# Gated graph phase: node rows from three split fp32r products, tiles in pairs, 512-column elementwise instructions

## The reference, cut to what matters

```
t   = relu(nf @ W1.T + b1)            # one row of 256 per node: "rows"
s   = segment_sum(t[src], dst)        # sum over the incoming edges: "messages"
m   = s @ W2.T + deg * b2             # W2 is folded into W_ih ahead of the steps
r,z = sigmoid(...), n = tanh(...)     # GRU gates from m and nf: "gates"
nf  = (1 - z) * n + z * nf
```

## Time and profile before

| | |
|---|---|
| device time, three runs | 4059.73, 4059.72, 4056.88 us; median 4059.72 us |
| span of the profiled execution, first to last instruction | 4057.3 us |
| PE busy | 3711.8 us, 91% of the span |
| DVE, ACT, POOL busy | 62%, 38%, 19% |
| granted clock of PE, mean over the span | 0.959 of full speed |

### The profile page before, as it was taken

One profiled execution on the slowest core, in us unless ns is written; L12 is line 12 of the kernel. 1 busy time (PEld: TensorE's weight loads), 2 busy tenths in 40 slices (PEclk: granted clock), 3 DMA queues, 4 the chain that ended last, 5 costly groups with the idle time before them and its releaser, 6 DMA issues. The chain is left out here.

```text
span 4057.3 us, 61050 instructions
## 1 busy us (share of the span) xinstructions
PE 3711.8 (91%) x18981; PEld 3087.0 (76%) x18981; DVE 2525.8 (62%) x5060; ACT 1533.3 (38%) x3578; POOL 758.0 (19%) x614
## 2 busy tenths in 40 slices
PE   5996879999999999999998799787999999779996
PEld 2554459989899899898997688655888888758884
DVE  7774755555555555555554555544777777577775
ACT  0363211121211211212112544334888886135553
POOL 0000000000000000000000200003888885012221
PEclk9997989999999999999999899898999999779998
DMA  1364112222222222222221211012333332411113
GB/s 41 64 102 87 48 50 78 87 67 85 76 79 86 74 80 87 67 85 76 79 85 40 66 30 31 13 41 61 93 93 93 94 93 68 177 44 35 38 35 116
DMA packets 297743, 288.61 MB, mean 71 GB/s; under 512 B 101485, under 2 KB 272847, under 8 KB 296806
## 3 DMA queue, kind: packets, MB, share of 16 engines
q1 hardware_dynamic: 233867, 208.29, 17.8%
q0 software_dynamic: 56576, 66.41, 6.4%
q10 hardware_dynamic: 7002, 10.15, 0.7%
HBM read 241.89 MB, written 42.47 MB: 70 GB/s over the span
## 5 line engine op out<-in xcount | busy, mean ns | idle before, releaser
L974 PE MATMUL bank<-a_wide,parts 125*128 125x448 f32 x4200 | 871.5, 367 | 0.1
L974 PEld LDWEIGHTS bank<-a_wide,parts 125*128 125x128 f32 x4200 | 785.7, 188 | 77.2 <-issue 10.1
L2205 POOL DMA_INDIRECT rows<-h_dram,src_t x400 | 493.5, 1234 | 124.1 <-DVE prod L2394 87.3
L2321 ACT ACTIVATE hot<-eq,ea 125x80 f32<-125x80 f32 x1600 | 413.2, 350 | 0.0
L949 POOL TENSOR_TENSOR nf_g<-nf,nf_g 128x896 fp32r<-128x896 f32 x42 | 94.5, 2249 | 1525.4 <-ACT nf_g L1112 1525.4
L1024 DVE CAST a_wide<-a_cols 125x2240 fp32r<-125x2240 bf16 x210 | 274.5, 1324 | 156.5 <-PE bank L974 141.0
L983 PE MATMUL bank<-nf_g,whh 128*128 128x448 f32 x1512 | 339.6, 369 | 0.0
L983 PE MATMUL bank<-msg,wc 128*128 128x448 f32 x1512 | 338.9, 368 | 0.0
L2247 PEld LDWEIGHTS bank<-prod,hot 125*80 125x80 f32 x2400 | 294.6, 150 | 54.1 <-issue 0.7
L2247 PE MATMUL bank<-prod,hot 125*80 125x128 f32 x2400 | 327.9, 273 | 0.0
L1117 ACT ACTIVATE msg<-bank 128x448 fp32r<-128x448 f32 x84 | 41.1, 542 | 702.6 <-PE bank L974 702.6
(11 more groups left out here) (431 smaller groups left out, 5894.4 us busy)
## 6 DMA issues: line engine op xcount, KB each, us to landing
a_cols<-a_dram SPq DMA_DIRECT2D x210, 546.9 KB
a_dram<-a_cols SPq DMA_DIRECT2D x15, 1250.0 KB, 10.9
w<-in_w SPq DMA_DIRECT2D x4, 2728.0 KB
deg_bc<-deg_dram SPq DMA_DIRECT2D x42, 224.0 KB, 6.1
gate_bc<-gate_dram SPq DMA_DIRECT2D x42, 224.0 KB, 3.2
rows<-h_dram,src_t POOLq DMA_INDIRECT x400, 4.2
w<-y_rows SPq DMA_DIRECT2D x12, 512.0 KB, 10.1
w<-in_w SPq DMA_DIRECT2D x5, 1024.0 KB
```

Of the source, the lines that this page charges most:

```text
L974: ins = nc.tensor.matmul(p_msg[f][:, 0:GW], parts[0:SPB, m, c * HB + k, f * 128:(f + 1) * 128], a_wide[u % 2][0:SPB, k, :], start=(c == 0 ...
L2205: nc.gpsimd.indirect_dma_start(out=rows[n % ITC][:, :], out_offset=None, in_=h_dram, in_offset=bass.IndirectOffsetOnAxis(ap=src_t[:, n:n + ...
L2321: ins = nc.scalar.activation(hot[:, q % 2, j, m, :], eq[:, q % 2, j, :], ACT.Copy, scale=ea4[:, q * UC + j, m:m + 1])
```

## The change

Row tiles are handled in pairs: ten pairs of early tiles, and three late entries (two pairs and the last tile alone). For each pair

- ACT copies the two tiles' columns of `nf` to fp32r (`nf_r[0]`, 128x500), POOL subtracts this from `nf` (`nf_r[1]`), and PE makes the three-term product of `nf_r` and a `w1` that is split into `w1[0]` and `w1[1]` in the weights phase. PE has 6 fp32r products of 256 columns for a tile, where it had 2 fp32 products;
- bias, relu and remainder are one instruction each for both tiles, 512 columns wide instead of 256.

`nf_r` and `t_raw` have two buffers, each for a pair. PE now waits for POOL's part (`row_low`) where it waited for `nf` itself. In ACT's list the copy of pair i stands ahead of the relu of pair i-1. The core of the diff:

```diff
@@ norm_and_gate_weights, the ends of POOL's and ACT's lists
+                pool.wait_ge(rest_in, START + 80)
+                pool.wait_ge(w1_high, START + 1)
+                nc.gpsimd.tensor_tensor(w1[1][:, :, :], w1_raw[:, :, :], w1[0][:, :, :], ALU.subtract)
...
+                act.wait_ge(rest_in, START + 80)
+                nc.scalar.activation(w1[0][:, :, :], w1_raw[:, :, :], ACT.Copy).then_inc(w1_high, 1)
@@ gated_graph, pairs
+    early, late = ([(k, min(k + 2, b)) for k in range(a, b, 2)] for a, b in ((0, EARLY * HB), (EARLY * HB, KT)))
@@ POOL
+                    def rows(s, some):
+                        for a, b in some:
+                            i = s * NPAIR + pairs.index((a, b))
+                            pool.wait_ge(row_high, START + i + 1)
+                            nc.gpsimd.tensor_tensor(nf_r[1][:, i % 2, :, 0:(b - a) * SPB], nf[:, :, a * SPB:b * SPB],
+                                                    nf_r[0][:, i % 2, :, 0:(b - a) * SPB], ALU.subtract).then_inc(row_low, 1)
...
+                        if g == 0:
+                            rows(s, late)
+                        if g == NGG - 1 and s < STEPS - 1:
+                            rows(s + 1, early)
@@ PE
-                            pe.wait_ge(nf_done, START + (s - 1) * NGG + min((k * SPB + SPB - 1) // GW + 1, NGG))
+                            pe.wait_ge(row_low, START + i + 1)
                             pe.wait_ge(t_sum, START + i - 1)
-                            for c in range(KD):
-                                ins = nc.tensor.matmul(p_t[i % 2][0:SPB, 0:D], nf[:, c, k * SPB:(k + 1) * SPB], w1[:, c, :],
-                                                       start=(c == 0), stop=(c == KD - 1))
+                            for h in range(b - a):
+                                terms = [(w1[m], nf_r[o], c) for m, o in ((0, 0), (0, 1), (1, 0)) for c in range(KD)]
+                                for j, (w_m, x_o, c) in enumerate(terms):
+                                    ins = nc.tensor.matmul(p_t[i % 2][0:SPB, h * D:(h + 1) * D], x_o[:, i % 2, c, h * SPB:(h + 1) * SPB],
+                                                           w_m[:, c, :], start=(j == 0), stop=(j == len(terms) - 1))
                             ins.then_inc(t_mm, 1)
@@ DVE
-                            dve.wait_ge(t_high, START + i - 3)
-                            dve.wait_ge(t_low, START + i - 3)
-                            nc.vector.tensor_tensor(t_raw[0:SPB, i % 4, :], p_t[i % 2][0:SPB, 0:D], b1_bc[0:SPB, :], ALU.add).then_inc(t_sum, 1)
+                            dve.wait_ge(t_high, START + i - 1)
+                            dve.wait_ge(t_low, START + i - 1)
+                            nc.vector.tensor_tensor(t_raw[0:SPB, i % 2, 0:b - a, :],
+                                                    p_t[i % 2][0:SPB, 0:(b - a) * D].rearrange("p (h d) -> p h d", d=D),
+                                                    b1_bc[0:SPB, :].rearrange("p (o d) -> p o d", o=1).broadcast_to((SPB, b - a, D)),
+                                                    ALU.add).then_inc(t_sum, 1)
@@ ACT
+                            act.wait_ge(nf_done, START + (s - 1) * NGG + min((b * SPB - 1) // GW + 1, NGG))
+                            act.wait_ge(t_mm, START + i - 1)
+                            nc.scalar.activation(nf_r[0][:, i % 2, :, 0:(b - a) * SPB], nf[:, :, a * SPB:b * SPB], ACT.Copy).then_inc(row_high, 1)
+                            if (a, b) != some[0]:
+                                relu(i - 1)
+                        relu(i)
+
+                    def relu(i):
+                        a, b = pairs[i % NPAIR]
+                        act.wait_ge(t_sum, START + i + 1)
+                        nc.scalar.activation(parts[0:SPB, 0, a:b, :], t_raw[0:SPB, i % 2, 0:b - a, :], ACT.Relu).then_inc(t_high, 1)
```

More of the change, by code:

```diff
@@ L168, in build @@
             ctx_w = ExitStack()
-            w1_g = sb(ctx_w, "w1_g", [128, KD, D])
+            w1_g = [sb(ctx_w, f"w1_g{m}", [128, KD, D], F32R) for m in range(PARTS)]
             wc = [sb(ctx_w, f"wc{m}", [128, KD, 3 * D], F32R) for m in range(PARTS)]
@@ L912, in gated_graph, with pairs_to @@
     EARLY = (NGG - 1) * GW // SPB // HB
+    early, late = ([(k, min(k + 2, b)) for k in range(a, b, 2)] for a, b in ((0, EARLY * HB), (EARLY * HB, KT)))
+    pairs = early + late
+    NPAIR = len(pairs)
+    def pairs_to(tile):
+        return next(i for i, (a, b) in enumerate(pairs) if b >= tile) + 1
     w1, wc, whh, b1_bc, b2, bih, bhh, bsum, b2c = gate_w
@@ L916, in gated_graph @@
         r_t, t_t, n_t, z_t = (shared[:, m * KD * GW:(m + 1) * KD * GW].rearrange("p (k n) -> p k n", k=KD) for m in range(4))
-        t_raw = sb(ctx, "t_raw", [128, 4, D])
+        t_raw = sb(ctx, "t_raw", [128, 2, 2, D])
+        nf_r = [sb(ctx, f"nf_r{m}", [128, 2, KD, 2 * SPB], F32R) for m in range(PARTS)]
         parts = sb(ctx, "parts", [128, PARTS, KT, D], F32R)
@@ L1002, in gates @@
                             gate(p_z, 1, f, False, wc, msg, True).then_inc(z_mm, 1)
-                    rows(0, range(EARLY * HB))
+                    rows(0, early)
                     for n in range(GR):
@@ L1008, in _ @@
                             if g == 0 and c == EARLY - 1:
-                                rows(s, range(EARLY * HB, KT))
+                                rows(s, late)
                             messages(s, n, c)
                         if g == NGG - 1 and s < STEPS - 1:
-                            rows(s + 1, range(EARLY * HB))
+                            rows(s + 1, early)
                         gates(n)
@@ L1100, in _, with rows @@
                 with act.If(crowded < 1):
-                    def rows(s, tiles):
-                        for k in tiles:
-                            i = s * KT + k
-                            act.wait_ge(t_sum, START + i + 1)
-                            nc.scalar.activation(parts[0:SPB, 0, k, :], t_raw[0:SPB, i % 4, :], ACT.Relu).then_inc(t_high, 1)
-                    rows(0, range(EARLY * HB))
+                    def rows(s, some):
+                        for a, b in some:
+                            i = s * NPAIR + pairs.index((a, b))
+                            act.wait_ge(nf_done, START + (s - 1) * NGG + min((b * SPB - 1) // GW + 1, NGG))
+                            act.wait_ge(t_mm, START + i - 1)
+                            nc.scalar.activation(nf_r[0][:, i % 2, :, 0:(b - a) * SPB], nf[:, :, a * SPB:b * SPB], ACT.Copy).then_inc(row_high, 1)
+                            if (a, b) != some[0]:
+                                relu(i - 1)
+                        relu(i)
+                    def relu(i):
+                        a, b = pairs[i % NPAIR]
+                        act.wait_ge(t_sum, START + i + 1)
+                        nc.scalar.activation(parts[0:SPB, 0, a:b, :], t_raw[0:SPB, i % 2, 0:b - a, :], ACT.Relu).then_inc(t_high, 1)
+                    rows(0, early)
                     for n in range(GR):
```

32 lines of the change are left out of this document (17 added, 15 removed).

## The result

The changed kernel takes 4106.8 us (median of 4 runs, 4105.35 to 4108.85) where the kernel before took 4059.4 (4 runs, 4056.88 to 4059.73). The ratio is 1.0122, interval 1.0107 to 1.0136: 1.2% slower. The forecast was 4120 with a range of 4096 to 4150.

What follows compares the result with a forecast made beforehand. PE was taken to bound the graph phase (busy 1606.9 of 1622.8 us). Losses of 42 + 5 + 2 + 1.9 + 9 = 60 us on a span of 4057.3, 2.4 under the median, gave 4120 us, range 4096 to 4150.

Steps and rivals of the forecast that it cites:

- The ring: Rows: chain from PE's product through sum, relu, copy and subtract back to PE, 4.95 us a round of two pairs.
- The port: Rows: POOL's subtract and DVE's two-SBUF-input remainder exclude each other; a run ends 0.4 us later, 2.4 us in the total.
- Early rows of steps 1 to 5: Late start plus longer rounds: PE through at 850.7 instead of 842.4, 8.35 us a step, 42 for five.
- The clock: PE's gaps put one round in five at half clock: 1.5 us a step, 9 in all.
- Step 0: Early rows of the first step, at half clock at first: end at 592.0 against 587.2, 5 us lost.
- Late rows: Last tile alone goes round the chain once: 4.90 us against 4.55, six times 0.35 is 2 us.
- Weights phase: Split of `w1` on ACT and POOL behind ACT's last copy, ahead of a barrier: 1.9 us.
- PE as the bound: Rival in the rows: ACT and POOL keep ahead, a round is 2.84 us, total 4053 us; chance 6%.
- POOL at its median: Rival in the rows: POOL's subtract takes 1.717 us, not its least, total 4136 us; chance 14%.

Runs made afterwards that it cites:

- experiment 1: Changed kernel with ACT's copy of pair i+1 ahead of the relu of pair i-1: +18.1 us against the kernel before, ratio 1.0046.
- experiment 5: Changed kernel with four pair buffers instead of two and ACT's copies three pairs ahead of the relu: +4.9 us against the kernel before, ratio 1.0010.
- experiment 9: Changed kernel with every POOL subtract of the rows made twice, values unchanged: +129.0 us against the kernel before, ratio 1.0323.
- experiment 2: Changed kernel with ACT's copies of the first two early pairs ahead of the messages' copies, at once: +45.8 us against the kernel before, ratio 1.0112.
- experiment 3: Changed kernel with pairs and 512-column instructions only; plain fp32 product, no copy, subtract or W1 split: -9.8 us against the kernel before, ratio 0.9977.
- experiment 4: Changed kernel with the three-term product on single tiles, 256-column instructions, two one-tile buffers: +121.4 us against the kernel before, ratio 1.0308.
- experiment 7: Changed kernel with four buffers and four copies ahead of the messages' copies, behind the fourth message chunk: -25.0 us against the kernel before, ratio 0.9940.
- experiment 10: Changed kernel, two buffers, copy ahead of the previous pair's relu, first two copies behind the fourth message chunk: 0.0 us against the kernel before, ratio 1.0002.
- experiment 6: Changed kernel with the first two early copies ahead of the messages' copies but behind the fourth message chunk: +37.0 us against the kernel before, ratio 1.0089.

## Why the prediction was right, term by term

**The ring was right, link by link.** 4.95 forecast, 4.89 measured. The single links stand within 0.15: PE's start to the sum 1.73 for 1.60 (the products are 0.118 apart as taken, but the second one behind a wait starts 0.22 behind the first, so that twelve take 1.69 to the last one's end and not 1.57; DVE follows 0.04 later), POOL 1.16 for 1.24, POOL to PE 0.05 for 0.14, the rest within 0.03. The errors cancel in part. Experiments 1, 5 and 9 each change one part of it and the round follows, by the link's length and by what the port adds: without the sum and the relu in the ring it is 4.10, with twice the buffers 3.80, with a second subtract 6.14.

**The port was right in kind.** Every second remainder is 1.08 long where 0.68 is its free length, since POOL's subtract is under way, and the sum is never held. Where it costs time had only been named for the end of a run; experiments 1, 2 and 5 show that it costs time as soon as the ring is opened. The forecast's words that an instruction with a single SBUF input is free do not hold for all: in experiment 2 DVE's widening, which has one, took 2.28 us for 1.33 while POOL subtracted.

**Early rows of steps 1 to 5: 42 forecast, 45.4 measured at one bad round.** Start 2.97 us (3.16 forecast), run 23.95 against 17.83, 9.1 a step, and one of the five runs (step 4) 1.3 longer. But the 45.4 hold the clock's loss, which was a term of its own: each run of 23.9 us is 0.95 above what its rounds take at 4.89. Without it a step costs 8.15 where 8.35 was forecast.

**The clock: 9 forecast, about 6 measured.** A dip came in every run, as taken, but cost 0.95 and not 1.5, since only part of a round is slow; in step 4 two rounds are slow, which cost 1.3 more. The slow round is the first one in steps 1 and 2 and the second in steps 3 and 5, at a clock of 0.67 to 0.71. One round in five had been assumed, no row gave it: that it came so is luck, and in us this is the term that was mis-sized most.

**Step 0: 5 forecast, 2.7 measured** (36.04 for 33.34), at a clock of 0.84 over its first 23 us. The pairs win there what experiment 3 shows, 1.6 us, which the forecast did not count.

**Late rows: 2 and 2.** 4.88 to 4.90 in all six, with two errors that cancel: the last tile starts 4.08 behind the first (4.19 forecast) and takes 0.81 (0.71).

**Weights phase: 1.9 forecast;** 2.36 from one point to the next, 1.83 by the start of the rows.

**Not in the sum:** the gates' products take 3.1 us less over the phase (14.78 a group for 14.85) and the messages around the late rows 1.4 less. Part of it goes with the plain fp32 product: PE's first twelve gate products behind the rows take 2.47 us to the next (855.90 to 858.37) where they took 2.64 behind plain fp32 products (842.37 to 845.01), and 40 messages behind the late rows take 8.16 for 8.34; experiment 3, with plain fp32 products, has 2.65 and 8.35. That is 1 us of the gates and the messages' 1.4. The other 2 us of the gates come neither from the product nor from the pairs: a group away from the rows takes 14.88 in the kernel before (14.41 in three cases) and 14.78 at full clock in every other trace here, experiments 3 and 4 among them. Their cause is open.

Measured so: 45.4 + 1.3 + 2.7 + 2.0 + 1.8 - 3.1 - 1.4 = 48.7, and the spans differ by 49.8. The forecast's 60 was too high by 4.3 for the early rows with their clock (42 + 9 for 46.7), by 2.3 for step 0, and by these 4.5. (The links of the ring as listed add up to 4.94 and not 4.95, which changes nothing.)

Of the rivals, PE as the bound fell with the changed trace (round 4.89, not 2.9); it needs four buffers, another order and early copies (experiment 7), and then gives -25. POOL at its median fell too: 1.16 in the ring. POOL's slow subtracts are seen only where the ring is shorter or the copies come early.

## What to carry to other kernels

When a product's input is made by other engines from a small ring of buffers, write down the ring from PE's start back to PE's start with its handoffs and divide by the buffers: that, and not PE's cheaper work, is the pace if it is longer. Then look at where the first instruction of the ring stands in each engine's list; here the order was worth 29 us (experiment 1), two more buffers 13 (5 against 1) to 25 (7 against 10), an early start 10 (6) to 30 (7 against 5), and the cheaper product itself 15 (7 against 3). An early start that falls into another engine's work was worth nothing (2). Put work for GpSimd where VectorE has no instruction with two SBUF inputs, or the time moves to VectorE and comes back to PE from there.

## What the runs showed of the hardware

- A GpSimd subtract of 128x500 takes 1.16 us alone and 1.55 to 1.6 when it starts while DVE runs an instruction with two SBUF inputs (0.68 us). In the other direction, while POOL subtracted, DVE's last instruction of the blend took 1.94 where it takes 1.09 alone, and the widening of columns, with one SBUF input, 2.28 where it takes 1.33 (experiment 2; two in 3.51).
- 12 fp32r products of 256 columns take 1.68 us (to the last one's end) at the higher of PE's two clock levels, 2.4 GHz, and 2.92 at 1.2 GHz. In the changed kernel one part of each run is at the lower level, also when PE goes from the messages to the rows without a wait (experiment 6: clock 0.92 over 828 to 850). In experiment 7, where PE has no waits in the run, it stayed at 1.00; in experiment 10, with none at the start and waits of 0.1 to 0.7 us in the rounds, too; in experiment 1, with such waits but 2.81 us at the start, it fell to 0.71 over the first 5 us; in experiment 9, with 2.8 us of waits in a round, it was at 0.55 to 0.70 over three of the five runs, and in the other two back at 1.00 after the first rounds (0.86 and 0.85 over the run).
- The second of PE's products behind a wait starts 0.22 us behind the first, the later ones 0.118 (changed kernel, 842.68 to 844.37). Behind plain fp32 products, twelve gate products take 2.64 us to the next, behind fp32r ones 2.47.
